# Graph network kernel, first layer's edge loop: one window of 224 nodes per edge tile, leaky sums on VectorE, and own loads ahead of own stores

## What is computed

```python
src = concatenate([edge_index[0], loop]); dst = concatenate([edge_index[1], loop])
xl = (x @ Wl).reshape(n, H, C)            # H = 4 heads of C = 32
xr = (x @ Wr).reshape(n, H, C)
m = xl[src] + xr[dst]
e = leaky_relu(m, 0.2)
logits = einsum('ehc,hc->eh', e, att)
amax = segment_max(logits, dst)
ex = exp(logits - amax[dst]); denom = segment_sum(ex, dst)
out = segment_sum(ex / denom[dst] * xl[src], dst)
```

## Time and profile before

| | |
|---|---|
| median of 3 runs | 3507.84 us (3499.35 to 3516.61) |
| the profiled execution | 3512.0 us, span 3510.2 |
| TensorE busy | 3011.9 us, 86% of the span |
| VectorE busy | 2482.2 us, 71% |
| ScalarE busy | 1716.1 us, 49% |
| GpSimd busy | 1647.1 us, 47% |
| moved | 637.66 MB, mean 182 GB/s |
| mean granted TensorE clock | 0.959 of full |
| own stage | from about 45 to 457 us |
| edge loop | from about 482 to 1171 us |
| a load of x (256 KB), all stages | 4.2 us from issue to landing, median |

### The profile page before, as it was taken

The page is one execution under the profiler, slowest core; times in us unless marked ns, Lnnn a source line. Parts: engine busy times, 40 slices in busy tenths (PEclk is TensorE's granted clock), DMA queues, the critical chain, the costliest instruction groups (busy, mean ns, idle before and its releaser), DMA issues.

```text
span 3510.2 us, 68649 instructions
## 1 busy us (share of the span) xinstructions
PE 3011.9 (86%) x17947; PEld 2215.3 (63%) x17947; DVE 2482.2 (71%) x7956; ACT 1716.1 (49%) x4046; POOL 1647.1 (47%) x2010
## 2 busy tenths in 40 slices
PE   4666679999999588879979999979998999996997
PEld 3666668888888455458865555547884555555665
DVE  5666646666666588878867777764446777776998
ACT  2333323333333244449985666644444666664665
POOL 0000055555555022227767777741227777763555
PEclk9999989999999799999999999999999999998999
DMA  5666667777777388869963333338983333337997
GB/s 129 192 183 189 189 154 165 167 168 165 165 166 162 90 244 237 240 202 293 293 230 94 105 103 104 104 86 273 301 287 100 103 103 103 104 98 242 343 330 262
DMA packets 804343, 637.66 MB, mean 182 GB/s; under 512 B 81661, under 2 KB 682066, under 8 KB 803954
## 3 DMA queue, kind: packets, MB, share of 16 engines
q1 hardware_dynamic: 599874, 396.49, 39.8%
q0 software_dynamic: 54208, 130.20, 13.9%
q10 hardware_dynamic: 149872, 106.57, 10.1%
HBM read 398.80 MB, written 234.13 MB: 180 GB/s over the span
## 4 chain that ended last, share of the span: by engine, by line
PE 28%; POOL 22%; issue 12%; DVE 12%; DMA 11%; ACT 9%; ACTq 3%; SPq 2%; DVEq 0%; POOLq 0%
POOL work L900 22%; DMA work<-in_x_dram 5%; PE bank L981 4%; ACT work L1371 4%; PE bank L978 3%; DMA work<-w_d 3%; PE bank L1179 3%; PE bank L1186 3%; PE bank L991 3%; PE bank L992 3%; PE bank L967 2%; PE bank L966 2%; ACT work L1363 1%; ACTq L463 1%; DVE seg_max L1726 1%
## 5 line engine op out<-in xcount | busy, mean ns | idle before, releaser
L2023 DVE SCALAR_TENSOR_TENSOR work<-bank,coef,work 128x128 f32<-128x128 f32 x2400 | 674.0, 342 | 245.2 <-ACT work L1405 241.8
L1132 PE MATMUL bank<-basis_s,work 128*128 128x512 f32 x1600 | 756.0, 595 | 1.5 <-ACT work L1398 1.5
L858 POOL DMA_INDIRECT work<-xl_d,slot_src x400 | 382.4, 956 | 740.5 <-issue 540.7
L900 POOL DMA_INDIRECT work<-x_d,slot_src x400 | 384.1, 960 | 126.3 <-issue 121.6
L900 POOL DMA_INDIRECT work<-h_d,slot_src x400 | 385.1, 963 | 123.8 <-issue 121.6
L1405 ACT ACTIVATE work<-bank,coef 128x128 f32<-128x128 f32 x800 | 293.9, 367 | 224.7 <-PE bank L1132 224.7
L1132 PEld LDWEIGHTS bank<-basis_s,work 128*128 128x128 f32 x1600 | 274.3, 191 | 196.6 <-issue 192.6
L1143 PEld LDWEIGHTS bank<-work 128*126 128x126 f32 x1600 | 206.9, 189 | 101.6 <-issue 100.9
L1186 PEld LDWEIGHTS bank<-work 128*128 128x128 f32 x1552 | 205.8, 193 | 97.7 <-issue 92.8
L1179 PE MATMUL bank<-work,loop_s 128*128 128x512 f32 x392 | 212.8, 625 | 28.0 <-ACT work L1445 26.7
L872 POOL DMA_DIRECT2D conv_d<-work x99 | 73.8, 750 | 335.5 <-DVE work L1912 325.1
(11 more groups left out here) (278 smaller groups left out, 6895.5 us busy)
## 6 DMA issues: line engine op xcount, KB each, us to landing
w_d<-work SPq DMA_DIRECT2D x800, 62.5 KB
work<-in_x_dram SPq DMA_DIRECT2D x194, 256.0 KB, 4.2
work<-x_d SPq DMA_DIRECT2D x194, 256.0 KB, 4.6
w_d<-work SPq DMA_DIRECT2D x400, 66.9 KB
work<-w_d SPq DMA_DIRECT2D x398, 64.0 KB, 3.4
work<-w_d ACTq DMA_DIRECT2D x390, 64.0 KB, 3.5
xl_d<-work SPq DMA_DIRECT2D x97, 256.0 KB, 2.5
xr_d<-work SPq DMA_DIRECT2D x97, 256.0 KB, 3.1
```

The source lines that it names most:

```text
L858: pool.indirect_dma_start(gathered(i)[:, c, :], None, xl_d, bass.IndirectOffsetOnAxis(ap=slot_src[:, a:a + 1], axis=0)).then_inc(e_in[i % ...
L900: pool.indirect_dma_start(quad(0, i % 3)[:, c, :], None, (x1_d, h1_d)[l], bass.IndirectOffsetOnAxis(ap=slot_src[:, a:a + 1], axis=0)).then ...
L1132: pe.matmul(psum[YBANKS[k % 5]][:, :], quad(1, i % 2)[:, c, :], basis_s[:, l, :, :].rearrange("k b n -> k (b n)"), start=True, stop=True). ...
L2023: ins = dve.scalar_tensor_tensor(o, psum[YBANKS[k % 5]][:, b * D:(b + 1) * D], coef[:, i, l, c, b:b + 1], o, ALU.mult, ALU.add)
```

## The change

- **One window per tile.** WINDOW becomes 224 nodes, for all 125 edges of a tile. A window is loaded in two-row pieces: lane p holds rows 2p and 2p + 1, so it takes LANES = 112 lanes of 1024 bytes. SP issues all four windows of a row; ScalarE's queue issues none.
- **Even and odd one-hots.** `turn_matrix(i)` compares the relative numbers with 2p and with 2p + 1 (`lane_two`), two passes of 112 x 500. `mix(i)` multiplies each with its half of the window: two products of 125 columns per tile in place of one of 63 and one of 62.
- **Leaky sums on VectorE.** ScalarE evicts m once, as a copy. The new `leaky(i)` on VectorE makes max(0.2 m, m) from it, and `logits(i)` has one matmul per tile. Semaphore `lr_ok` takes the place of `m_cp` ahead of the logits.
- **VectorE's order in a row** becomes turn_matrix(i+2), maxima(i), leaky(i+1), values(i), slot_matrix(i+1), hot_types(i) if due.
- **Own stage.** SP's loop over q is `load_own(q + 3)` and then `save_own(q)`.

The core of the diff:

```diff
-HALF = (TE + 1) // 2
-WINDOW = 112
-HALVES = ((0, HALF), (HALF, TE))
+WINDOW = 224
+LANES = WINDOW // 2
...
-                eng.dma_start(window(h, i)[0:WINDOW, c, :], xr_d[bass.ds(at, WINDOW), :]).then_inc(window_in[i % 3], 16)
+                eng.dma_start(window(c, i), xr_d[bass.ds(at, WINDOW), :].rearrange("(p h) d -> p h d", h=2)).then_inc(window_in[i % 3], 16)
...
             for q in range(QUADS):
-                save_own(q)
                 if q + 3 < QUADS:
                     load_own(q + 3)
+                save_own(q)
...
-                    for h, (a, b) in enumerate(HALVES):
-                        last = pe.matmul(both[:, c * P + 1 + a:c * P + 1 + b], window(h, i)[0:WINDOW, c, :],
-                                         turned_pick(i)[:, c, a:b], start=False, stop=h == 1, skip_group_check=True)
+                    for h in range(2):
+                        last = pe.matmul(both[:, c * P + 1:c * P + 1 + TE], window(c, i)[:, h, :],
+                                         turned_pick(h, i)[:, c, :], start=False, stop=h == 1, skip_group_check=True)
...
-                pe.wait_ge(m_cp, i + 1)
+                pe.wait_ge(lr_ok, i + 1)
...
-                    pe.matmul(logit_t, att_heads[:, c, :], quad(8, i % 2)[:, c, :], start=c == 0, stop=False)
-                    last = pe.matmul(logit_t, att_heads[:, c, :], quad(14, i % 2)[:, c, :], start=False, stop=c == CHAINS - 1)
+                    last = pe.matmul(logit_t, att_heads[:, c, :], quad(14, i % 2)[:, c, :], start=c == 0, stop=c == CHAINS - 1)
...
-                act.activation(flat(8, i % 2), psum[i % 2][:, :], ACT.Relu, scale=1.0 - SLOPE)
-                act.activation(flat(14, i % 2), psum[i % 2][:, :], ACT.Copy, scale=SLOPE).then_inc(m_cp, 1)
+                act.activation(flat(8, i % 2), psum[i % 2][:, :], ACT.Copy).then_inc(m_cp, 1)
...
-                dve.tensor_scalar(turned_pick(i), row.rearrange("p (c e) -> p c e", c=CHAINS), lane_p[0:WINDOW, 0:1], None,
-                                  ALU.is_equal).then_inc(pt_ok, 1)
+                for h in range(2):
+                    last = dve.tensor_scalar(turned_pick(h, i), row, lane_two[0:LANES, h:h + 1], None, ALU.is_equal)
+                last.then_inc(pt_ok, 1)
+
+            def leaky(i):
+                dve.wait_ge(m_cp, i + 1)
+                if i >= 2:
+                    dve.wait_ge(lg_ps, i - 1)
+                dve.scalar_tensor_tensor(flat(14, i % 2), flat(8, i % 2), SLOPE, flat(8, i % 2), ALU.mult, ALU.max).then_inc(lr_ok, 1)
...
             for i in range(ROWS):
-                if i % 4 == 0:
-                    hot_types(i)
-                maxima(i)
                 if i + 2 < ROWS:
                     turn_matrix(i + 2)
+                maxima(i)
+                if i + 1 < ROWS:
+                    leaky(i + 1)
                 values(i)
                 if i + 1 < ROWS:
                     slot_matrix(i + 1)
+                if i % 4 == 0:
+                    hot_types(i)
```

More of the change, by code:

```diff
@@ L211, in gnn_kernel @@
         drop_t = sb("drop_t", [CHAINS * H, 2, BLOCK, P])
-        base_f = sb("base_f", [ROWS, 2, CHAINS])
-        base_at = sb("base_at", [ROWS, 2 * CHAINS], I32)
-        far_at = sb("far_at", [P, 2, CHAINS])
+        base_f = sb("base_f", [ROWS, CHAINS])
+        base_at = sb("base_at", [ROWS, CHAINS], I32)
+        far_at = sb("far_at", [P, CHAINS])
+        lane_two = sb("lane_two", [P, 2])
         half_id = sb("half_id", [P, TE])
@@ L436, in gathered, with window, turned_pick, load_windows @@
             return quad((0, 5)[i % 6 // 3], i % 3)
-        def window(h, i):
-            return quad((1, 6)[h], i % 3)
+        def window(c, i):
+            at = i % 3 * 512 + c % 2 * 2 * D
+            return work[(1, 6)[c // 2]][0:LANES, at:at + 2 * D].rearrange("p (h d) -> p h d", h=2)
         def relative(b):
             return work[(7, 11)[b % 2]][:, 0:BLOCK * CHAINS * TE // 2].bitcast(BF16)
-        def turned_pick(i):
-            return quad(9, i % 3)[0:WINDOW, :, 0:TE]
-        def load_windows(eng, h, i):
+        def turned_pick(h, i):
+            k, s = (9, i % 3) if h == 0 else ((10, 10, 12)[i % 3], (0, 1, 0)[i % 3])
+            return quad(k, s)[0:LANES, :, 0:TE]
+        def load_windows(eng, i):
             if i >= 3:
                 eng.wait_ge(mx_ps, i - 2)
-            row = base_at[i:i + 1, h * CHAINS:(h + 1) * CHAINS]
             starts = nc.values_load_multi_w_load_instructions(
-                row, engines=[eng.engine], min_val=0, max_val=N + EPAD - WINDOW,
+                base_at[i:i + 1, :], engines=[eng.engine], min_val=0, max_val=N + EPAD - WINDOW,
                 skip_runtime_bounds_check_because="a window lies before the last node, or in the rows set out edge by edge")[1]
             for c, at in enumerate(starts):
-                eng.dma_start(window(h, i)[0:WINDOW, c, :], xr_d[bass.ds(at, WINDOW), :]).then_inc(window_in[i % 3], 16)
+                eng.dma_start(window(c, i), xr_d[bass.ds(at, WINDOW), :].rearrange("(p h) d -> p h d", h=2)).then_inc(window_in[i % 3], 16)
         def load_packed(eng, l, q, first, last):
@@ L660, in _ @@
             for i in range(3):
[L661 removed]
+                load_windows(sp, i)
                 if i < 2:
@@ L799, in _ @@
             pool.memset(neg_half[:, :], -0.5).then_inc(consts, 1)
-            pool.iota(far_at[:, :, :], [[HALF, 2], [ROWS * TE, CHAINS]], base=N, channel_multiplier=TE,
+            pool.iota(far_at[:, :], [[ROWS * TE, CHAINS]], base=N, channel_multiplier=TE,
                       allow_small_or_imprecise_dtypes=True).then_inc(consts, 1)
-            for a, b in HALVES:
-                pool.iota(half_id[:, a:b], [[1, b - a]], base=0, channel_multiplier=0,
-                          allow_small_or_imprecise_dtypes=True).then_inc(consts, 1)
+            pool.iota(half_id[:, :], [[1, TE]], base=0, channel_multiplier=0,
+                      allow_small_or_imprecise_dtypes=True).then_inc(consts, 1)
+            pool.iota(lane_two[:, :], [[1, 2]], base=0, channel_multiplier=2,
+                      allow_small_or_imprecise_dtypes=True).then_inc(consts, 1)
             pool.sem_inc(consts, 1)
@@ L1278, in _ @@
                 own_projected(q)
-            act.wait_ge(pos_ok, 2)
-            act.wait_ge(nodes_ready, 1)
-            for i in range(3):
-                load_windows(act, 1, i)
             edges_mixed(0)
@@ L1517, in _ @@
             st.wait()
-            spans = base_f[:, :, :]
-            for h, (a, b) in enumerate(HALVES):
-                st.did(dve.tensor_tensor(spans[:, h, :], raw[:, 1, :, b - 1], raw[:, 1, :, a], ALU.subtract))
+            st.did(dve.tensor_tensor(base_f[:, :], raw[:, 1, :, TE - 1], raw[:, 1, :, 0], ALU.subtract))
             st.wait()
-            for h in range(2):
-                st.did(dve.tensor_scalar(backward[:, :, TE + h], spans[:, h, :], float(WINDOW) - 0.5, None, ALU.is_gt))
+            st.did(dve.tensor_scalar(backward[:, :, TE], base_f[:, :], float(WINDOW) - 0.5, None, ALU.is_gt))
             st.wait()
@@ L1707, in turn_matrix @@
                     dve.wait_ge(mx_ps, i - 2)
[L1708 to L1710 removed]
+                row = relative(b)[0:LANES, i % BLOCK * CHAINS * TE:(i % BLOCK + 1) * CHAINS * TE].rearrange("p (c e) -> p c e", c=CHAINS)
+                for h in range(2):
[6 more added lines that the diff above has]
+                dve.scalar_tensor_tensor(flat(14, i % 2), flat(8, i % 2), SLOPE, flat(8, i % 2), ALU.mult, ALU.max).then_inc(lr_ok, 1)
             def maxima(i):
@@ L1774, in _ @@
             turn_matrix(1)
+            leaky(0)
             for i in range(ROWS):
-                if i % 4 == 0:
-                    hot_types(i)
-                maxima(i)
                 if i + 2 < ROWS:
                     turn_matrix(i + 2)
+                maxima(i)
+                if i + 1 < ROWS:
+                    leaky(i + 1)
                 values(i)
```

28 lines of the change are left out of this document (11 added, 17 removed).

## The result

The changed kernel takes 3309.46 us, median of 4 runs (3306.09 to 3313.63), against 3512.23 (3499.35 to 3522.06) for the kernel before on the same chip: a ratio of 0.9425, with a 95% interval of 0.9391 to 0.9460. The profiled execution took 3309.04 us, its span 3307.1.

A forecast was written before the change was run, and what follows sets the result against it. The prediction took the own stage as bound by a loop through the load of x, the edge loop by TensorE's chain; gains of 98 + 39 = 137 us from 3507.84 gave 3371 us, range 3320 to 3440.

The forecast's parts named there:

- the value between the ends: Own stage: 3.2 us a quad instead of 4.20, gaining 98 us; ends 2.92 (125 us) and 3.7 (49 us).
- the rival of 7 us: Own stage: reordered loads meet full queues and take 7 us, quads stay at 3.7 us; 3420 us, chance 0.13.
- Edge loop, the mix: TensorE's mix grows from 2.86 to 3.30 us a row (3.01 to 3.54), at 0.125 us per 125-column instruction.
- my own formulas: Edge-loop row times: plain 1.42 + 0.29 + 3.30 + 0.98 = 5.99 us, with coefficients 7.00, with type transposes 6.49.
- the good-ends rival of 3322: Own stage and edge loop both reach their good ends, gaining 125 + 61 us; 3322 us, chance 0.12.
- Edge loop, the logits and the order: Logits fall from 1.86 to 0.98 us; one-hots move into VectorE's wait, out of the chain; the leaky pass costs nothing.
- Type row: Edge loop: VectorE's type one-hots (0.87 us) make one row in four 6.42 us.
- the margin that I gave as 0.44 us: Edge loop, plain row: VectorE's 5.55 us of work is 0.44 us less than TensorE's 5.99.
- the rival at 3408: Edge loop: the leaky pass stands aside for a gather issue of 0.96 us, VectorE bounds, edge gain gone; chance 0.11.
- is not in the chain: Edge loop: ScalarE drops one of two evictions and its window issues; it was said not to be in the chain.
- its place is unchanged: Edge loop: SP issues four windows and four stores a row as before, so its place was said to be unchanged.
- My rival of a loop at the lower level: Edge loop: TensorE's clock falls to 1.2 GHz; with half the rows there 3599 us, chance 0.03.

The follow-up runs named there:

- e1: The changed kernel with the load order undone: SP stores quad q before loading quad q+3; 3430.54 us.
- e2: The kernel before with only the load order changed: SP loads quad q+3 before storing quad q; 3391.24 us.
- e11: The changed kernel without the third of VectorE's four passes per quad in the own stage (self logits wrong); 3286.11 us.
- e6: The changed kernel with window products cut to their first 63 columns (other edges lack their target part); 3313.48 us.
- e3: The changed kernel with leaky sums back on ScalarE (two evictions) and eight logit matmuls a row; 3371.02 us.
- e4: The changed kernel with the one-hots of row i+2 behind the maxima of row i again; 3327.82 us.
- e5: The changed kernel with ScalarE issuing the windows of tiles 2 and 3 ahead of its compaction, SP the others; 3331.52 us.
- e8: The kernel before with the change's load order, leaky sums and VectorE order, but its own 112-node windows, half issued by ScalarE; 3336.55 us.
- e13: The changed kernel with ScalarE issuing the windows of tiles 2 and 3 of row i+4 behind its exponentials, SP the others; 3296.77 us.

## Why the prediction was right in kind and wrong in size

**Own stage.** The loop through the load was what bound it, and three quads per round in place of two freed it: e1 and e2 show it alone at 121 and 118 us. I forecast 98. The step that failed is the value between the ends: I took 3.2 us a quad for slow loads and rounds at the low clock, and it is 3.0. The low-clock rounds that I had priced were a product of the old loop: with TensorE waiting less, the clock rose to 0.98, and e1 and e2 show that it goes with the load order alone (0.89 and 0.99). Loads did lengthen, from 3.6 to 4.0 us on the median, but the rival of 7 us didn't come. That VectorE's passes would stand next was right; the transfers are less near than I thought (2.8 us a quad in e11, not 2.92).

**Edge loop, the mix.** This is the term that was mis-sized most. I had 0.125 us for an instruction of 125 columns and left the identity pair at 0.28, so 3.30. Measured are 0.11 and 0.23: 0.42 + 3 x 0.23 + 16 x 0.11 = 2.87. The nearer row was the 128 x 128 product of the logits (0.11), not the sum product of 137 columns; and an identity pair that I priced from a mix with narrow neighbours is shorter next to wide ones. Window product and identity pair together take 0.67 us a tile before and after, though columns double, and e6 at 63 columns takes no less time. With 2.87 my own formulas give 5.56 for a plain row (5.57 measured), 6.57 with coefficients (6.46) and 6.06 with the type transposes (5.95). The lower end of the range for the mix, 3.01, was too high too (16 x 0.11 with the other terms as I had them makes 3.06), and with it the good-ends rival of 3322.

**Edge loop, the logits and the order.** 1.86 to 0.98 was right (0.99). That the leaky pass costs VectorE nothing was right only while VectorE has a margin: e3 loses 0.9 us on three rows, and 0.35 on the type row, where VectorE sets the time. e3's 62 us and e4's 18 us say which of the two parts is the larger.

**VectorE.** Type row: 6.42 forecast, 6.10 measured. Counted up to the start of the next pass, the two one-hots of that row show 0.78 us, not 0.92, the type one-hots 0.79, not 0.87, and values and slot matrix 2.53, not 2.63: I had added up passes from start to end, and they overlap a little. In plain rows the margin that I gave as 0.44 us fell to almost nothing as the mix came out shorter: VectorE is last in half the rows.

**VectorE stretched beside gathers, the rival at 3408.** It didn't come for the leaky pass: 670 ns beside the gathers, 692 in the own stage, which has none. Other passes are longer than before: the one-hot pass takes 555 ns on the mean, 462 before, and a gather's issue 1006 ns, 955 before. The 555 are of two kinds: 60 of the 161 passes last about 700 ns, the others 461 to 481. That these 60 stand aside for gathers fits, but no run took the gathers away.

```profile
L1700 DVE TENSOR_SCALAR work<-work,lane_two 112x500 f32<-112x500 bf16 x161 | 82.7, 555 | 1.2 <-DMA work<-rel_d 1.1
L1707 DVE SCALAR_TENSOR_TENSOR work<-work 128x512 f32<-128x512 f32 x81 | 54.2, 670 | 0.3 <-issue 0.3
```

```profile
L861 POOL DMA_INDIRECT work<-xl_d,slot_src x327 | 329.0, 1006 | 171.1 <-DVEq L1748 93.2 <-issue 77.8
```

The Trainium skill (GPSIMD Engine Reference, Specifications) names two kinds of VectorE instruction that contend with GpSimd: those with two SBUF inputs, and those in a 2-port performance mode. For the first, this case's trace disagrees (670 against 692 ns). Whether the one-hot, which reads bf16 and has one tensor input, is of the second kind no row here shows.

**ScalarE "is not in the chain".** It is true of after, since the change takes ScalarE's issues away, and I gave that no price. e5 shows that two of them ahead of the compaction would have cost 22 us in the new loop (e8, with four of half the size and the narrow windows, 27): with TensorE's row at 5.6 us and VectorE nearly full, the exponentials may not be late.

**SP, "its place is unchanged".** This sentence was wrong in kind. SP has the same eight issues in a row, but the row is shorter. It now issues the windows 7.3 us after their buffer is free, not 1.3, and in 15 of 81 rows TensorE's mix begins only as they land. The late rows cost 10 us, which made the gain smaller, not larger, and e13 recovers them.

**TensorE's clock.** 0.99 in the loop on the mean; between 400 and 900 us it falls in two of the four late rows alone, 42 and 78. My rival of a loop at the lower level didn't come.

**The sum.** With a stage of 3.0 us a quad (118) and a mix of 2.87 (row mean 6.15, 72 us) the same sum gives 190. That 6.15 meets the measured 6.14 is in part luck: the type row that I had 0.32 us too long (8 us in 25 rows) stands against the late rows that I didn't have (10 us). The rest of the 203: some 5 us at the start of the loop, where the time from the first mix to the first maxima fell from 14.1 to 9.5, and 7 us in the stage behind it, whose instructions are the same. For these 7 I have no cause: its clock reads 0.95 instead of 0.94, and no experiment looked at it.

## What to carry to other kernels

When a loop through a transfer serves more tiles per round, don't add slack for slow rounds that the old loop itself caused; a starved TensorE's low clock goes away with the starvation. Before costing a matmul by its columns, look whether its rows of half and double width differ at all. When a change shortens a row, ask of each queue how long it waits now, even if its own work stays: SP waited 80.5 us of 500 before and 36.5 after, and its windows came late. And ask which instruction stands ahead of the one that others wait for: two window issues on ScalarE cost 22 us in one place of its program, 28 in the next and gained 13 in the same place with one row more of lead.

## What I had not expected of the hardware

- Window products of 63 and 125 columns with 112 rows and 128 weights cost the kernel the same (3313 and 3309 us); 264 and 277 ns for one record.
- A VectorE pass with two operands in SBUF is not longer beside gathers (670 and 692 ns). One with a single bf16 operand went from 462 to 555 ns on the mean when it moved to another place in the row, with 60 of 161 passes at about 700, and gathers issue slower (955 to 1006 ns).
- 1.03 us of idle TensorE ahead of a mix was followed by 6 us at a granted clock of 0.50; windows that landed late so cost row 42 some 4.2 us. Idle times of 1.19 and 1.15 us ahead of the mixes at 752.21 and 791.49 were not: the next 6 us read 1.00.
- With pieces of 512 bytes the DMA engines read full at 282 GB/s; with 2 KB pieces they moved 292 GB/s at a share of 0.88.
